# A repeated SyncE list in another order: first output weights, then loads, then the maxima's rows, and one swapped pair on ScalarE

## The chip, the core and the metric

The kernel runs on one core of a Trainium2 chip (trn2), and all of its work is one program. The metric is the device time of one execution in microseconds (us). What the measurement of this kernel can tell from no change is about 0.2%, some 2 us.

## The reference

Sixteen sequences of 256 tokens with 256 features go through four residual blocks. Cut to what matters here:

```python
x = x + einsum(x, weight[subject]) + bias[subject]                 # L0, weights chosen per sequence
x = x + zX * lap_x(x) + zY * lap_y(x) + zR * x * (1 - x)           # L1
x = x + attention(x, side, seq_len) @ Wo + bo                      # L2, 16 heads, masked softmax
s0, s1 = dense(x, swi[0], swo[0]), dense(x, swi[1], swo[1])        # L3, two shared experts
eo = relu(x @ wi[label]) @ wo[label]                               # and one chosen per sequence
w = softmax(relu(concat(eo[0], s0[0], s1[0]) @ g1) @ g2)
x = x + eo * w[0] + s0 * w[1] + s1 * w[2]
```

## The kernel before, in words

Each engine works through a list of named stages written out by hand (lines 53 to 78: `PE_BODY`, `ACT_BODY`, `DVE_BODY`, `POOL_BODY`, `SP_BODY`). An opening with lists of its own is followed by a loop over the turns i = 2 to 15, and then turns 16 and 17, in which the stages that have no sequence left are left out. One turn holds work of three sequences: the function `lag` says how far behind a stage is. `load`, `x_parts` and the other early stages are of sequence i, the attention (`S0` to `S15`, `m0`, `m1`, `E0` to `E15`) of sequence i-1, and the experts (`H0` to `H11`, `P0` to `P11`, `wi0` to `wi3`, `wo0` to `wo3`, `sum`) of sequence i-2.

The engines keep to their own lists and wait for each other by semaphores. An engine that waits holds back everything behind it in its list.

What the names of this case do:

- `load` on SyncE (SP) looks up the sequence's subject in a table in SBUF (`chooser`, line 478, a TENSOR_LOAD and register work), waits until the transfers of the last turn have read the buffers, and issues five loads: `w0_raw` (line 481; the trace calls this buffer w_raw), `x_raw` (471), `s_raw` (474), and two small ones (484, 485).
- `wo0` to `wo3` on SP each look up the chosen expert's number anew (line 478), wait until GpSimd (POOL) has finished with the quarter n of the staging buffer `raw` in this turn (its input weights, stage `wi`n), and issue one load of 256 KB into that quarter (line 494). `wi_load` fills the four quarters with the next sequence's input weights (489).
- `m0` and `m1` on SP wait until ScalarE (ACT) has copied the transposed maxima of eight heads into `max_rows` (ACT's stage of the same name, line 997), and then issue the transfer of these rows into `q_rows` (539). PE's scores `E0` to `E7` need the first transfer (line 774), `E8` to `E15` the second.
- On ACT, `wo`n and `wi`n make the high part of a quarter (`exp_hi`, line 1027), and POOL makes the low part (`exp_lo`, 1364). `x_parts`, `w_parts` and `s_parts` make the high parts of what `load` brought (929, 932, 935). `H`n is the relu of a hidden bank (1049). `P3` copies an expert's output (1034). `E`h is two exponentials of a bank of scores (1006, 1010); the end of the second one frees the bank for PE.
- On PE, `S`, `m` and `E` and the other front stages use two PSUM banks in turn, by their order in `PE_BODY`. `E0`, `E1` and `E2` share one bank and `S12`, `S13` the other one, so that `E1` on PE waits for ACT's second exponential of `E0`, and `E2` for that of `E1`. The function `open_bank` sets these waits. All other engines' lists stay as they are.

Of the kernel before, what the change touches and what calls it, by code (L numbers as in the profile page):

```python
# [60 lines left out]
vs aT ks gate wo logits vp self  # L61
""".split()
ACT_BODY = """
H0 wi0 H1 x3_keep wi1 H2 wi2 wi3 H3 m0 wo0 H4 P3 wo1 x_parts H5 E0 w_parts wo2 E1 H6 E2 wo3 E3 H7 E4 E5 E6 m1 H8 s_parts E7
x1_parts react P7 q E8 H9 E9 x2_parts qa E10 E11 H10 E12 kp E13 E14 E15 H11 qb kq P11
aT vs ks x3_parts logits vp x2b sum
""".split()
# [6 lines left out]
wi0 wi1 wi2 wi3 wo0 m0 x_parts wo1 E0 w_parts wo2 E2 wo3 E4 E6 s_parts x1 E8 m1 E9 E10 qa E12 norm E15 qb ks vp sum  # L74
""".split()
SP_BODY = """
load wo0 wo1 wo2 m0 wo3 m1 wi_load E15 kp k3 sum
""".split()

S_OF, E_OF = [f"S{h}" for h in range(H)], [f"E{h}" for h in range(H)]  # L80
# [1428 lines left out]
```

## Time and profile before

| | us |
|---|---|
| median of 3 runs (1006.3 to 1008.48) | 1006.84 |
| the profiled execution's own time | 1013.26 |
| its span in the profile | 1011.4 |
| PE busy in the span | 979.8 |
| DVE, ACT, POOL busy | 792.5, 686.3, 636.5 |

The profiled execution is 6.4 us longer than the median of the timed runs, and its span covers all but 1.9 us of it. A turn of the loop takes some 59.2 us. Times in the trace are from the span's start. In the waits, the instruction named first is the one that waited, then who released it, the sum in us, how often, and the longest.

### The profile page before, as it was taken

What the parts mean: (1) busy time and instruction counts of PE and PEld (TensorE: products, weight loads), DVE (VectorE), ACT (ScalarE), POOL (GpSimd) and SP (SyncE); (2) the same over time, 40 slices, a digit from 0 to 9 for tenths busy, and PEclk for the clock granted to TensorE, in tenths of its full rate; (3) what the DMA queues carried; (4) which work ended last, traced back from release to release, by engine and by line L of the source; (5) the groups of instructions that cost most, each with busy time, mean ns of one, the idle gap of its engine ahead of it and who ended that gap; (6) DMA issues with size and microseconds to landing.
All of it is one profiled execution on the core that took longest, in us unless ns stands there. A gap on an engine that the chain in (4) does not pass through costs nothing.

```text
span 1011.4 us, 27951 instructions
## 1 busy us (share of the span) xinstructions
PE 979.8 (97%) x9604; PEld 932.6 (92%) x9604; DVE 792.5 (78%) x1558; ACT 686.3 (68%) x1443; POOL 636.5 (63%) x546
## 2 busy tenths in 40 slices
PE   8889999999999999999999999999999999999896
PEld 7679999999999999999999999999999999999796
DVE  5877878878788787878878787887878788888533
ACT  4766858667685876768587676857767685776541
POOL 4867747576684757658575765856576585656450
PEclk8889999999999999999999999999999999999988
DMA  6533132223213222331322233133222313221110
GB/s 196 150 105 106 50 111 73 63 84 100 88 43 110 77 63 84 94 94 42 104 84 63 84 88 100 42 97 90 63 84 79 109 42 92 84 75 55 43 52 11
DMA packets 92028, 82.70 MB, mean 82 GB/s; under 512 B 12100, under 2 KB 90980, under 8 KB 92004
## 3 DMA queue, kind: packets, MB, share of 16 engines
q1 hardware_dynamic: 91572, 81.99, 27.7%
q10 hardware_dynamic: 432, 0.39, 0.1%
q8 instruction: 15, 0.25, 0.1%
q14 instruction: 9, 0.07, 0.0%
HBM read 52.59 MB, written 4.20 MB: 56 GB/s over the span
## 4 chain that ended last, share of the span: by engine, by line
POOL 35%; issue 29%; PE 26%; DVE 3%; ACT 2%; SPq 1%; DMA 1%; POOLq 1%; DVEq 0%; ACTq 0%
POOL prob_lo L1428 11%; POOL exp_lo L1364 9%; PE out L652 3%; PE out L653 3%; PE out L654 3%; PE hid L652 2%; PE hid L653 2%; PE hid L654 2%; POOL p_lo L1381 2%; POOL s_lo L1381 2%; PE front L652 2%; PE front L654 2%; PE front L653 2%; POOL beside L1384 2%; POOL ksT L1395 2%
## 5 line engine op out<-in xcount | busy, mean ns | idle before, releaser
L652 PE MATMUL hid<-x_hi,exp_hi 128*128 128x256 f32 x768 | 231.5, 301 | 1.5 <-DVE x_lo L1250 1.5
L1428 POOL TENSOR_TENSOR prob_lo<-prob,prob_hi 128x512 f16<-128x512 f32 x143 | 185.0, 1294 | 74.3 <-ACT prob_hi L1010 74.1
L652 PE MATMUL out<-hid_hi,exp_hi 128*128 128x256 f32 x768 | 226.6, 295 | 0.1
L653 PE MATMUL hid<-x_lo,exp_hi 128*128 128x256 f32 x768 | 217.2, 283 | 0.0
L654 PE MATMUL hid<-x_hi,exp_lo 128*128 128x256 f32 x768 | 216.7, 282 | 0.0
L653 PE MATMUL out<-hid_lo,exp_hi 128*128 128x256 f32 x768 | 214.6, 279 | 0.0
L654 PE MATMUL out<-hid_hi,exp_lo 128*128 128x256 f32 x768 | 214.5, 279 | 0.0
L1364 POOL TENSOR_TENSOR exp_lo<-raw,exp_hi 128x512 fp32r<-128x512 f32 x128 | 168.8, 1334 | 72.1 <-ACT exp_hi L1027 72.0
L1170 DVE TENSOR_REDUCE s_max<-front 128x2 f32<-128x512 f32 x247 | 163.3, 688 | 61.6 <-PE front L760 59.6
L1049 ACT ACTIVATE hid_hi<-hid 128x512 fp32r<-128x512 f32 x192 | 114.9, 598 | 96.3 <-PE hid L654 94.4
L1006 ACT ACTIVATE prob<-front 128x512 f32<-128x512 f32 x246 | 147.5, 600 | 24.0 <-PE front L774 22.3
L1254 DVE SCALAR_TENSOR_TENSOR hid_lo<-hid,hid_hi 128x512 fp32r<-128x512 f32 x192 | 131.1, 683 | 37.0 <-ACT hid_hi L1049 35.5
L652 PEld LDWEIGHTS hid<-x_hi,exp_hi 128*128 128x128 f32 x768 | 145.7, 190 | 4.5 <-DVE x_lo L1250 1.6
L652 PEld LDWEIGHTS out<-hid_hi,exp_hi 128*128 128x128 f32 x768 | 144.5, 188 | 2.5 <-DVE hid_lo L1254 0.3
L653 PEld LDWEIGHTS hid<-x_lo,exp_hi 128*128 128x128 f32 x768 | 146.2, 190 | 0.0
L654 PEld LDWEIGHTS hid<-x_hi,exp_lo 128*128 128x128 f32 x768 | 145.6, 190 | 0.0
L653 PEld LDWEIGHTS out<-hid_lo,exp_hi 128*128 128x128 f32 x768 | 144.8, 189 | 0.0
L654 PEld LDWEIGHTS out<-hid_hi,exp_lo 128*128 128x128 f32 x768 | 144.3, 188 | 0.0
L1010 ACT ACTIVATE prob_hi<-front 128x512 f16<-128x512 f32 x230 | 137.8, 599 | 0.0
L774 PE MATMUL front<-q_rows,k_rows 100*128 100x256 bf16 x492 | 118.5, 278 | 3.8 <-DMA q_rows<-max_rows 2.0
L1190 DVE TENSOR_TENSOR prob_lo<-prob,prob_hi 128x512 f16<-128x512 f32 x113 | 104.2, 922 | 17.9 <-ACT prob_hi L1010 16.7
L1027 ACT ACTIVATE exp_hi<-raw 128x512 fp32r<-128x512 f32 x128 | 79.2, 632 | 23.4 <-DMA raw<-in_wo 23.4
(241 smaller groups left out, 2334.6 us busy)
## 6 DMA issues: line engine op xcount, KB each, us to landing
raw<-in_wi SPq DMA_DIRECT2D x64, 256.0 KB, 3.7
raw<-in_wo SPq DMA_DIRECT2D x64, 256.0 KB, 2.8
q_rows<-w_raw SPq DMA_DIRECT2D x80, 128.0 KB, 2.4
k_rows<-x_raw SPq DMA_DIRECT2D x48, 128.0 KB, 2.4
k_rows<-x1T SPq DMA_DIRECT2D x45, 128.0 KB, 2.4
x_raw<-in_x SPq DMA_DIRECT2D x16, 256.0 KB, 2.9
w_raw<-in_w SPq DMA_DIRECT2D x16, 256.0 KB, 2.7
s_raw<-in_side SPq DMA_DIRECT2D x16, 256.0 KB, 3.7
```

The lines of the kernel that those rows point to most:

```text
L652: nc.tensor.matmul(acc, w_hi, a_hi, start=first, stop=False)
L653: nc.tensor.matmul(acc, w_hi, a_lo, start=False, stop=False)
L654: return nc.tensor.matmul(acc, w_lo, a_hi, start=False, stop=last)
L774: last = nc.tensor.matmul(psum[:, k * S:(k + 1) * S], k_rows[0:ROWS_EXP, h, k * P:(k + 1) * P], q_rows[0:ROWS_EXP, h, :], start=True, stop ...
L1006: last = nc.scalar.activation(prob[:, h % NPROB, :], psum[:, :], ACT.Exp, scale=SCALE)
L1010: last = nc.scalar.activation(prob_hi[:, h % NPROB, :], psum[:, :], ACT.Exp, scale=SCALE)
L1049: nc.scalar.activation(hid_hi[:, s % 2, :], hid_bank[s % 2][:, :], ACT.Relu).then_inc(hid_hi_done, 1)
L1170: nc.vector.tensor_reduce(s_max[:, :, h:h + 1], psum, AX_X, ALU.max).then_inc(freed["S"], 1)
L1190: nc.vector.tensor_tensor(prob_lo[:, h % NPROB, :], prob[:, h % NPROB, :], prob_hi[:, h % NPROB, :], ALU.subtract).then_inc(prob_split_dve, 1)
L1254: nc.vector.scalar_tensor_tensor(hid_lo[:, s % 2, :], hid_bank[s % 2][:, :], 0.0, hid_hi[:, s % 2, :].bitcast(F32), ALU.max, ALU.subtract) ...
L1364: nc.gpsimd.tensor_tensor(lo, source, hi.bitcast(F32), ALU.subtract).then_inc(w_split, 1)
L1428: nc.gpsimd.tensor_tensor(prob_lo[:, h % NPROB, :], prob[:, h % NPROB, :], prob_hi[:, h % NPROB, :], ALU.subtract).then_inc(prob_split_poo ...
```

## The change

In ACT's repeated list `x_parts` and `wo1` change places. In SP's repeated list `wo0` goes ahead of `load`, and `m0` goes ahead of `wo1` and `wo2`. The opening's lists stay, and so does every stage's code.

```diff
 ACT_BODY = """
-H0 wi0 H1 x3_keep wi1 H2 wi2 wi3 H3 m0 wo0 H4 P3 wo1 x_parts H5 E0 w_parts wo2 E1 H6 E2 wo3 E3 H7 E4 E5 E6 m1 H8 s_parts E7
+H0 wi0 H1 x3_keep wi1 H2 wi2 wi3 H3 m0 wo0 H4 P3 x_parts wo1 H5 E0 w_parts wo2 E1 H6 E2 wo3 E3 H7 E4 E5 E6 m1 H8 s_parts E7
 ...
 SP_BODY = """
-load wo0 wo1 wo2 m0 wo3 m1 wi_load E15 kp k3 sum
+wo0 load m0 wo1 wo2 wo3 m1 wi_load E15 kp k3 sum
 """.split()
```

## Rows read from the trace of the kernel before

**Rows 1.** First part of the page: busy time, share and instructions.

```profile
PE 979.8 (97%) x9604; PEld 932.6 (92%) x9604; DVE 792.5 (78%) x1558; ACT 686.3 (68%) x1443; POOL 636.5 (63%) x546
```

**Rows 2.** Busy time of each engine in one turn, granted clock, DMA share, GB/s.

```profile
499.10:558.30 59.20, 59.04 (x594) 56.51 (x593) 48.78 (x97) 42.05 (x89) 39.03 (x34) 1.00 0.28 80
```

**Rows 3.** Waits of PE and its weight loads, turns 2 to 15.

```profile
PEld front L774 <- DMA q_rows<-max_rows: 2.3, 4, 1.4
PE front L774 <- DMA q_rows<-max_rows: 1.2, 1, 1.2
```

**Rows 4.** SP in order of time, head of a turn: start, us, instruction.

```profile
501.09 0.40 SPq L481 DMA_DIRECT2D w_raw<-in_w  x1
...
503.28 0.34 SPq L485 DMA_DIRECT2D z_sb<-in_z  x1
504.56 2.78 SPq L494 DMA_DIRECT2D raw<-in_wo  x3
507.48 0.86 SPq L539 DMA_DIRECT2D q_rows<-max_rows  x1
509.67 0.39 SPq L494 DMA_DIRECT2D raw<-in_wo  x1
```

**Rows 5.** ACT in order of time, same turn; in brackets the idle time before.

```profile
505.30 0.37 ACT L997 ACTIVATE max_rows<-front 24x256 bf16<-24x256 bf16 x1 [1.34 <-PE front L766]
...
507.42 0.63 ACT L1027 ACTIVATE exp_hi<-raw 128x512 fp32r<-128x512 f32 x1 [1.64 <-DMA raw<-in_wo]
...
508.79 0.66 ACT L1034 ACTIVATE e_out<-out 128x256 f32<-128x256 f32 x2 [0.25 <-PE out L654]
509.34 0.63 ACT L1027 ACTIVATE exp_hi<-raw 128x512 fp32r<-128x512 f32 x1
509.86 0.63 ACT L929 ACTIVATE x_hi<-x_raw 128x512 fp32r<-128x512 f32 x1
...
513.34 0.62 ACT L1010 ACTIVATE prob_hi<-front 128x512 f16<-128x512 f32 x1
```

**Rows 6.** PE in order of time, same turn: the matmuls of E1 and E2.

```profile
512.14 0.39 PE L774 MATMUL front<-q_rows,k_rows 100*128 100x256 bf16 x2
...
514.02 0.39 PE L774 MATMUL front<-q_rows,k_rows 100*128 100x256 bf16 x2
```

**Rows 7.** SP's line 478 between wo0 and wo1, and between m0 and wo3 (ns).

```profile
L478 SPq TENSOR_LOAD <-label_sb x1: 272/272/272, 505.0 to 505.0; - x1
...
L478 SPq TENSOR_LOAD <-label_sb x1: 732/732/732, 508.4 to 508.4; - x1
```

**Rows 8.** Issue to landing: wo3 and wo2 of this turn, all 64 issues (line 494).

```profile
raw<-in_wo SPq DMA_DIRECT2D x1, 256.0 KB, 2.7
...
raw<-in_wo SPq DMA_DIRECT2D x1, 256.0 KB, 3.1
...
DMA to landing us min/median/max: 2.5/2.8/3.8
```

**Rows 9.** Turn 3 in order of time: ACT's last exponential of E1, PE's E2.

```profile
157.87 0.63 ACT L1010 ACTIVATE prob_hi<-front 128x512 f16<-128x512 f32 x1
...
158.55 0.39 PE L774 MATMUL front<-q_rows,k_rows 100*128 100x256 bf16 x2
```

**Rows 10.** POOL in order of time, the low parts of wi0 to wi3.

```profile
498.90 5.00 POOL L1364 TENSOR_TENSOR exp_lo<-raw,exp_hi 128x512 fp32r<-128x512 f32 x4
```

**Rows 11.** Turn 2: SP's last small load, ACT's maxima, PE's E2.

```profile
87.43 1.42 SPq L485 DMA_DIRECT2D z_sb<-in_z  x1
...
89.36 0.37 ACT L997 ACTIVATE max_rows<-front 24x256 bf16<-24x256 bf16 x1 [1.35 <-PE front L766]
...
99.35 0.39 PE L774 MATMUL front<-q_rows,k_rows 100*128 100x256 bf16 x2
```

**Rows 12.** Turn 16: ACT's maxima and the relu of H5.

```profile
920.25 0.37 ACT L997 ACTIVATE max_rows<-front 24x256 bf16<-24x256 bf16 x1 [1.26 <-PE front L766]
...
925.39 0.60 ACT L1049 ACTIVATE hid_hi<-hid 128x512 fp32r<-128x512 f32 x1 [0.47 <-PE hid L654]
```

## The prediction

> **What bounds the kernel now.** I read the busy shares first: TensorE (PE) is busy for 979.8 of 1011.4 us, the other engines for 792 us and less [rows 1]. The busy time by turn says the same of the loop: 59.04 of 59.20 us, at the full granted clock of 1.00 (2.4 GHz), while POOL works for 39 us and ACT for 42 [rows 2]. So the kernel is PE's own list, one matmul behind the other. Anything that comes earlier on another engine is worth only what PE now waits for it, and anything that comes later costs as soon as PE's small reserves are used up.
>
> What PE waits for is in the waits. In turns 2 to 15 its weight loads wait four times for the maxima's rows, 2.3 us together, 1.4 of them in turn 2 (PE itself 1.2) and 0.3 in three other turns [rows 3]. ACT's much longer wait, 1.64 us in each turn for wo0 [rows 5], makes nobody late: right after it ACT waits 0.25 us for PE again, before P3's output.
>
> Then the timelines of SP, ACT and PE side by side, since the change moves DMA issues against ACT's work. **ACT has almost no reserve at E1 and E2.** E2's matmuls start at 514.02 [rows 6], and the exponential that frees their bank ends at 513.34 + 0.62 = 513.96 [rows 5]. In turn 3 the same exponential ended at 158.50 and E2 started at 158.55, later than its turn in PE's list would have let it [rows 9]. So I take 0.05 us from an ACT end to the start of what waits for it, and E2's reserve is nearly nothing.
>
> **wo0 ahead of the loads.** It takes the place of w0 at 501.09 [rows 4]. What it must wait for, POOL's low part of wi0, is the first of four from 498.90 on, each 1.25 us, so done at 500.15 [rows 10]: no wait. It lands 3.5 us earlier, and ACT's 1.64 us of idle time goes. Worth nothing: ACT then waits for P3's output from PE instead.
>
> **The loads behind it.** One look-up and issue of a wo costs SP (2.78 - 0.38) / 2 = 1.20 us, an issue itself 0.38 [rows 4]. The five loads go 1.2 us later, the last one issued by 503.28 + 0.34 + 1.2 = 504.8. With the longest landing of any wo, 3.8 us [rows 8], all are there by 508.6, before ACT's x_hi, which comes at 509.34 at the earliest. Cost nothing. If that cover is gone, a late x_raw costs one for one, as wo1 does below.
>
> **The maxima's rows.** SP is free at 504.8, and ACT releases it at 505.30 + 0.37 = 505.67 [rows 5]. They are issued at 505.72 instead of 507.48 [rows 4], 1.8 us earlier. All of PE's wait for them goes: 0.3 us in three turns, and the one of turn 2.
>
> **wo1 and wo2 behind the rows: here is the price.** Before, wo1 was issued at about 505.76 (504.56 + 1.20), long before the rows. Now it can't be issued until ACT's m0 has released SP. From there:
> - rows issued 505.72 to 506.58 (0.86 us) [rows 4];
> - look-up and registers, 1.33 us, as between the rows' end at 508.34 and wo3 at 509.67 [rows 4]: wo1 issued at 507.91. The look-up there takes 0.73 us where it takes 0.27 behind a weight load [rows 7];
> - 2.76 us to ACT's start: wo3, issued alone behind the rows, lands in 2.7 [rows 8], and wo0 shows 0.06 more than the median landing until ACT starts (504.56 to 507.42: 2.86) [rows 4, 5]. So 510.67.
>
> ACT is ready for wo1 at 509.86, since **the swapped pair** puts x_parts into its place at 509.34 [rows 5] and hides 0.52 us. It idles 0.81 us. From wo1's start to the end of E1's last exponential ACT has a solid row of work: before, 509.34 to 513.96, less the 0.52 of x_hi that is now ahead of it: 4.10 us. So that end comes at 514.77 and E2 on PE at 514.82 instead of 514.02: **0.80 us lost in a turn.** E1's stall is part of this and not added. Behind E2 all is as before, only later: each engine takes its pace from PE and nothing gives it back.
>
> wo2 is issued at 509.11 and lands by 512.3 at 3.1 us [rows 8]; ACT wants it at 513.3 or so. wo3 at 510.3 is in time too. POOL's list is unchanged: it gets x_hi earlier and wo1 later and has 20 us of idle time in a turn [rows 2]; nothing.
>
> **The bounds of a turn's price.** With a look-up of 0.27 and a landing of 2.5 it is 0.80 - 0.46 - 0.20 = 0.14 us; with a landing of 3.1 it is 1.20, with 3.8 it is 1.90 [rows 7, 8]. I take 0.80, since both terms come from rows with the same neighbour, the transfer of the maxima's rows just ahead.
>
> The Trainium skill (DMA: Bandwidth & Descriptors, Anatomy of one DMA) gives 2.0 us and the bytes over 436 GB/s for a transfer, for a DMA issued by GpSimd; for 256 KB that is 2.6 us, an estimate. The trace has 2.7 for the nearest one, and by the skill's figure a turn would lose 0.1 us less.
>
> **The sum.**
> - turns 3 to 15: 13 x 0.80 = +10.4; three of them had a wait of 0.3 for the rows, which the new chain takes in: -0.9;
> - turn 2: released at 89.73, so E2 at 89.73 + 0.05 + 0.86 + 1.33 + 2.76 + 4.10 + 0.05 = 98.88 instead of 99.35, a gain of 0.47 [rows 11]. The last small load took 1.42 us there instead of 0.34, and with wo0 ahead SP may come to m0 up to 0.3 us late: I take -0.3;
> - turn 16, without x_parts to cover: released at 920.62, wo1 there at 925.62 by the same steps, H5 on ACT 0.52 later, 926.14 instead of 925.39 [rows 12]; less E1's small reserve +0.7;
> - turn 17 has no m0, no load: nothing.
>
> Together +9.9 us. The profiled execution (1013.26 us, span 1011.4) would come to 1023.2; its extra over the median belongs to both kernels, so the median goes from 1006.84 to 1016.7.
>
> **Rivals.**
> 1. *Faster: wo1 comes in time.* What decides is whether wo1 is there some 4.2 us after ACT's release (509.86 - 505.67); the rows give 5.0. If look-up and landing were both at their lower ends, 4.3, PE would keep its list, the waits for the rows would go, 1.2 + 0.9 = 2.1 us, and perhaps the last idle hundredths before E0: 1004.7. For it: that stall is real. Against: 0.73 us stands in the row with just this neighbour. Chance 0.06.
> 2. *The short look-up.* Only the look-up is 0.27: a turn loses 0.34, 13 x 0.34 - 0.9 - 0.8 + 0.2 = +2.9: 1009.7; with a landing of 2.6 too it comes within 0.2%. Chance 0.10 for the two, most of it above 0.2%. [...]
> 3. *More than a wait for one load:* wo1 shares the queue with wo2 and takes 3.1 us to land: 13 x 1.20 - 0.9 + 0.1 + 1.1 = +15.9, 1022.7. For it: wo2 took 3.1 with the rows behind it. Against: two loads were in flight ahead of wo2, and nothing is ahead of wo1. Chance 0.12.
> 4. *ACT isn't in the way.* Another buffer frees E1's bank, or the waits overlap so that the change does nothing: 1006.8. Against: turn 3's E2. Chance 0.05.
>
> My forecast keeps 0.67. The range takes in most of rival 2 and goes most of the way to rival 3: 1009.0 to 1021.5. A difference below 0.2% (2 us) couldn't be told from none. Faster 0.06, same 0.08, slower 0.86.
>
> **What would show it.** Right: ACT's waits no longer list exp_hi behind the transfer at wo0 but at wo1, about 0.8 us in each turn, with the row of idle time behind x_hi; PE waits for prob_hi at E1 or E2, 0.6 to 0.8 us, in 14 turns; a turn of 60.0 us; SP's rows 0.05 us behind ACT's max_rows; no wait for the rows. Wrong: no wait of ACT for raw behind x_hi, or a turn of 59.2 us or less. If ACT waits as said and PE doesn't, the step from ACT to E2 is what failed; if wo1's issue comes less than 2.2 us behind the release, it is the look-up.

## The result, and the profile after

| | before | after |
|---|---|---|
| median, us (runs; lowest to highest) | 1007.76 (6; 1006.3 to 1011.33) | 1017.59 (6; 1016.26 to 1019.96) |
| profiled execution, us | 1013.26 | 1018.05 |
| its span, us | 1011.4 | 1016.2 |
| 13 turns of the loop in that span, us | 770.50 | 778.41 |

The ratio is 1.0085 with a 95% interval of 1.0068 to 1.0103: slower by 0.85%, some 8.6 us, and clear of the 0.2% that can be told. The forecast was 1016.7 us, 9.9 us more than before. In this table the kernel before has six timed executions, the three of the first table among them.

The page's first part shows PE still as the bound, busy for 2.1 us less in a span that is 4.8 us longer:

```profile
PE 977.7 (96%) x9604; PEld 928.6 (91%) x9604; DVE 769.5 (76%) x1558; ACT 690.6 (68%) x1443; POOL 629.9 (62%) x546
```

One turn, busy time of each engine, clock, DMA share and GB/s, to be read beside [rows 2]: PE has 0.54 us of idle time where it had 0.16.

```profile
501.23:560.95 59.72, 59.18 (x594) 56.45 (x594) 47.00 (x97) 42.40 (x89) 38.42 (x34) 1.00 0.27 80
```

How long a turn is can be read from SP's store of the output (line 556), once a turn. Its first and its fourteenth start, 13 turns apart, in the kernel before:

```profile
143.63 0.42 SPq L556 DMA_DIRECT2D out<-e_out  x1
...
914.13 0.42 SPq L556 DMA_DIRECT2D out<-e_out  x1
```

and in the changed kernel:

```profile
141.76 0.42 SPq L556 DMA_DIRECT2D out<-e_out  x1
...
920.17 0.43 SPq L556 DMA_DIRECT2D out<-e_out  x1
```

770.50 / 13 = 59.27 us a turn before and 778.41 / 13 = 59.88 after: 0.61 us more, 7.9 in all. The span grew by only 4.8, since in this execution of before the stretch up to the first store was 1.9 us longer and the one behind the fourteenth 1.2. Those two stretches also differ between executions of one kernel: the first store of the kernel that was run twice, e10 and e12 (below), came at 141.27 and 142.93. So turns are compared below by 13 of them in the profile, and kernels by the timed ratio.

The waits of turns 2 to 15, PE and its weight loads, then ACT's for the transfers:

```profile
PE front L774 <- ACT prob_hi L1010: 7.8, 14, 1.1
PEld front L774 <- ACT prob_hi L1010: 13.1, 28, 1.3
...
ACT exp_hi L1027 <- DMA raw<-in_wo: 9.4, 15, 1.2
```

The wait for the maxima's rows [rows 3] is gone from these turns. In its place PE waits for ACT's exponential, once in each of 14 turns (its weight loads twice), and ACT's wait for the weights, 1.64 us before in the turn of [rows 5], is 9.4 us in 15 waits, 0.6 each, and it now stands at wo1 and no longer at wo0. SP at the head of a turn, as in [rows 4]:

```profile
503.21 0.41 SPq L494 DMA_DIRECT2D raw<-in_wo  x1
504.54 0.37 SPq L481 DMA_DIRECT2D w_raw<-in_w  x1
...
506.69 0.34 SPq L485 DMA_DIRECT2D z_sb<-in_z  x1
507.81 0.86 SPq L539 DMA_DIRECT2D q_rows<-max_rows  x1
510.00 2.82 SPq L494 DMA_DIRECT2D raw<-in_wo  x3
```

and ACT in the same turn, as in [rows 5]:

```profile
507.42 0.37 ACT L997 ACTIVATE max_rows<-front 24x256 bf16<-24x256 bf16 x1 [1.34 <-PE front L766]
...
510.90 0.66 ACT L1034 ACTIVATE e_out<-out 128x256 f32<-128x256 f32 x2 [1.35 <-PE out L654]
511.45 0.64 ACT L929 ACTIVATE x_hi<-x_raw 128x512 fp32r<-128x512 f32 x1
512.54 0.63 ACT L1027 ACTIVATE exp_hi<-raw 128x512 fp32r<-128x512 f32 x1 [0.46 <-DMA raw<-in_wo]
...
516.03 0.62 ACT L1010 ACTIVATE prob_hi<-front 128x512 f16<-128x512 f32 x1
```

PE's E1 and E2, as in [rows 6]:

```profile
514.69 0.39 PE L774 MATMUL front<-q_rows,k_rows 100*128 100x256 bf16 x2 [0.38 <-ACT prob_hi L1010]
...
516.70 0.39 PE L774 MATMUL front<-q_rows,k_rows 100*128 100x256 bf16 x2
```

The chain can be followed in these rows: ACT's max_rows ends at 507.79, SP issues the rows at 507.81 and wo1 at 510.00, ACT starts on it at 512.54 after 0.46 us of idle time, its last exponential of E1 ends at 516.65, and E2 starts at 516.70. From ACT's release to E2 that is 8.91 us; before it was 514.02 - 505.67 = 8.35.

This turn is the mildest of the loop. Over turns 3 to 15 the same stretch takes 8.91 to 9.18 us in the changed kernel, 9.05 on average. In the kernel before it is 8.34 to 8.37 us in ten of them and 8.52 to 8.58 in three. What varies in the changed kernel is wo1's landing: from its issue to ACT's start it takes 2.54 us here and up to 2.80, 2.67 on average. The slowest one, in the turn at 390 us:

```profile
390.09 2.80 SPq L494 DMA_DIRECT2D raw<-in_wo  x3
...
392.89 0.63 ACT L1027 ACTIVATE exp_hi<-raw 128x512 fp32r<-128x512 f32 x1 [0.72 <-DMA raw<-in_wo]
```

So the average turn pays 9.05 - 8.35 = 0.70 us at this place.

### The profile page after: what moved, and what is told of

It is laid out like the page before. It is cut to its first block, busy times and chain, and to the rows that moved or that the text cites. A ratio compares the mean times of both kernels' runs of the same rounds, so it can differ in the third digit from the quotient of the medians.

```text
span 1016.2 us, 27951 instructions
## 1 busy us (share of the span) xinstructions
PE 977.7 (96%) x9604; PEld 928.6 (91%) x9604; DVE 769.5 (76%) x1558; ACT 690.6 (68%) x1443; POOL 629.9 (62%) x546
## 4 chain that ended last, share of the span: by engine, by line
PE 35%; POOL 30%; issue 24%; ACT 3%; DVE 3%; DMA 2%; SPq 1%; POOLq 1%; ACTq 0%; DVEq 0%
POOL exp_lo L1364 10%; POOL prob_lo L1428 7%; PE out L652 3%; PE out L654 3%; PE out L653 3%; PE hid L652 3%; PE hid L653 3%; PE hid L654 3%; PE front L652 2%; PE front L654 2%; PE front L653 2%; PE front L774 2%; POOL beside L1384 1%; PE front L760 1%; DMA raw<-in_wo 1%
## 5 line engine op out<-in xcount | busy, mean ns | idle before, releaser
L1190 DVE TENSOR_TENSOR prob_lo<-prob,prob_hi 128x512 f16<-128x512 f32 x113 | 109.5, 969 | 19.0 <-ACT prob_hi L1010 17.7
L715 PE MATMUL pv<-v_cols,prob_hi 128*128 128x49 bf16 x1024 | 83.2, 185 | 4.6 <-DVE den L1201 2.0
```

Of the source, the lines that this page charges most:

```text
L1190: nc.vector.tensor_tensor(prob_lo[:, h % NPROB, :], prob[:, h % NPROB, :], prob_hi[:, h % NPROB, :], ALU.subtract).then_inc(prob_split_dve, 1)
```

## The experiments

All ratios are to the kernel before, which was timed again beside the runs (medians of 1008.2 to 1009.2 us). The length of a turn is 13 turns of the profile over 13, as above. For the kernel before that profile is of its slowest execution (1013.26 us), and its 59.27 us may be a little high: e5, which has the same list on SP, has 59.18.

| run | SP's head | ACT, PE's gate | ratio (95%) | a turn, us |
|---|---|---|---|---|
| before | load wo0 wo1 wo2 m0 wo3 | wo1 x_parts | 1 | 59.27 |
| the change | wo0 load m0 wo1 wo2 wo3 | x_parts wo1 | 1.0085 (1.0068 to 1.0103) | 59.88 |
| e1 | wo0 load wo1 wo2 m0 wo3 | as the change | 0.9975 (0.9964 to 0.9986) | 59.20 |
| e2 | load wo0 m0 wo1 wo2 wo3 | as the change | 1.0081 (1.0068 to 1.0094) | 59.93 |
| e3 | wo0 load wo1 m0 wo2 wo3 | as the change | 0.9972 (0.9961 to 0.9982) | 59.16 |
| e4 | as the change, one look-up | as the change | 0.9973 (0.9960 to 0.9985) | 59.16 |
| e5 | as before | x_parts wo1 | 0.9990 (0.9978 to 1.0002) | 59.18 |
| e6 | as the change | wo1 x_parts | 1.0159 (1.0137 to 1.0180) | 60.47 |
| e7 | as the change | wo1 behind E0 | 1.0061 (1.0039 to 1.0082) | 59.78 |
| e8 | as the change, wo1 looked up twice | as the change | 1.0173 (1.0148 to 1.0198) | 60.48 |
| e9 | as the change | w_parts ahead of H5, wo1 behind E0 | 1.0127 (1.0108 to 1.0146) | 60.17 |
| e10 | as before, one look-up | as before | 0.9999 (0.9988 to 1.0010) | 59.23 |
| e11 | e4 again | | 0.9977 (0.9966 to 0.9988) | 59.14 |
| e12 | e10 again | | 0.9987 (0.9976 to 0.9999) | 59.20 |

**Which move in SP's list costs.** Two runs undo one move each, the third puts only wo1 ahead of m0.

```diff
-wo0 load m0 wo1 wo2 wo3 m1 wi_load E15 kp k3 sum
+wo0 load wo1 wo2 m0 wo3 m1 wi_load E15 kp k3 sum    (e1)
+load wo0 m0 wo1 wo2 wo3 m1 wi_load E15 kp k3 sum    (e2)
+wo0 load wo1 m0 wo2 wo3 m1 wi_load E15 kp k3 sum    (e3)
```

Expected of e1:

> The change with m0 put back behind wo2 (SP: wo0, load, wo1, wo2, m0, wo3). Theory (the price is wo1 waiting for ACT's m0, then ACT, E1, E2): wo1 is issued some 0.9 us behind the last small load, before the rows, so ACT never waits for it; the rows go out as late as before. The loss of 0.6 us a turn is gone: ratio to before 1.000, within 0.002. Rival A (the cost is the loads coming 1.2 us later, or wo0's transfer among them): the order of wo0 and the loads is as in the change, so it stays near 1.0085.

Of e2:

> The change with wo0 back behind the loads (SP: load, wo0, m0, wo1, wo2, wo3). Theory: nothing of the price hangs on wo0's place, since SP reaches m0 at about the same time and waits there for ACT; ratio 1.0085, 0.6 us a turn, ACT's idle time at wo0 back in part. Rival A: the loss is gone, ratio near 1.000.

Of e3:

> The change with wo1 alone put ahead of m0 (SP: wo0, load, wo1, m0, wo2, wo3). Theory: wo1 is issued at about 505.8 on before's clock, the rows follow at 506.2 instead of 507.48 and wo2 at 508.4, there by 511.0 where ACT wants it at 512.3. No wait at ACT, none of PE for the rows: about 1 to 2 us faster than before, ratio 0.998 to 1.000. Rival B (whatever stands behind the rows pays, wo2 as well as wo1): wo2 late, a loss of 0.3 us or more a turn, ratio above 1.004.

With m0 back in its place the loss is gone (59.20 us a turn), with wo0 back in its place it is all there (59.93). wo0's place and the later loads cost nothing: rival A falls. The ratio of e1 came out below what was expected, 0.9975 against 1.000 within 0.002, and those of e3 and e4 too (0.9972 and 0.9973, where 0.998 was the lowest expected). In e1 the rows still go out as late as before, 1.79 us behind ACT's release (499.99 + 0.37), where it was 1.81:

```profile
502.15 0.87 SPq L539 DMA_DIRECT2D q_rows<-max_rows  x1
```

So early rows aren't what makes e1 faster than before.

e3 isolates the loss to one stage: wo1 ahead of m0 or behind it makes 0.72 us a turn (59.88 against 59.16). The SP rows of e3, and ACT's:

```profile
501.58 0.38 SPq L494 DMA_DIRECT2D raw<-in_wo  x1
502.10 0.87 SPq L539 DMA_DIRECT2D q_rows<-max_rows  x1
504.27 1.61 SPq L494 DMA_DIRECT2D raw<-in_wo  x2
```

```profile
505.19 0.64 ACT L929 ACTIVATE x_hi<-x_raw 128x512 fp32r<-128x512 f32 x1
505.71 0.63 ACT L1027 ACTIVATE exp_hi<-raw 128x512 fp32r<-128x512 f32 x1
```

wo1 is issued at 501.58, 4.1 us ahead of its use, and ACT goes from x_hi to it without a wait. The rows still go out 0.57 us behind ACT's release (501.16 + 0.37), early enough for PE, whose 13 turns are all between 59.13 and 59.18 us. wo2 behind the rows is no trouble: rival B falls.

**How much of it is the look-up.** e4 looks the expert's number up once, at wo0, and keeps it; e8 looks it up twice at wo1.

```diff
+            held = {}                                                 (ahead of SP's stages)
...
                     n = int(name[2])
-                    kind = chooser(label_sb, i, wo.shape[0])
+                    if n == 0:                                        (e4, e11; e10 and e12 in the old order)
+                        held["kind"] = chooser(label_sb, i, wo.shape[0])
+                    kind = held["kind"]
...
+                    if n == 1:                                        (e8, behind the first look-up)
+                        kind = chooser(label_sb, i, wo.shape[0])
```

Expected of e4:

> The change with one look-up of the expert's number for wo0 to wo3, at wo0, kept in a register. Theory: wo1 follows the rows by about 0.1 instead of 1.33 us, lands 1.2 us earlier, before ACT is ready for it; the loss is gone, ratio 0.998 to 1.001. Rival C (the price is the place behind the rows in the transfer queue, not SP's time): ratio stays near 1.008.

Of e8:

> The change with the look-up of wo1 done twice, a dose of SP time between the rows and wo1. Theory: the second look-up costs SP 0.5 to 0.8 us (0.27 the load, the rest registers), and since ACT and then PE have no reserve left the whole of it comes out in each of 14 turns: 7 to 11 us more than the change, ratio 1.015 to 1.020. Rival D: little or nothing more.

e4 keeps m0 ahead of wo1, and the loss is gone. Its SP rows (the lines have moved by two):

```profile
501.97 0.88 SPq L541 DMA_DIRECT2D q_rows<-max_rows  x1
503.13 1.66 SPq L496 DMA_DIRECT2D raw<-in_wo  x3
```

wo1 follows the rows' start by 1.16 us where it took 2.19 in the change. That falls short of the 0.1 us behind the rows' end that I expected (it is 0.28), and is enough: wo1 is ready in time. Rival C, the place behind the rows in the queue, falls with it. e8 is the same term the other way. From the rows' end to wo1 it has 1.93 us, 0.60 more than the 1.33 of the change:

```profile
509.87 0.87 SPq L539 DMA_DIRECT2D q_rows<-max_rows  x1
512.67 1.61 SPq L494 DMA_DIRECT2D raw<-in_wo  x2
```

and a turn has 60.48 instead of 59.88 us, 0.60 more. The chain passes SP's time on one for one, and rival D falls. The two look-ups themselves, in ns as shortest, median, longest:

```profile
L478 SPq TENSOR_LOAD <-label_sb x2: 268/518/769, 510.8 to 511.9; - x2
```

The first behind the rows takes 0.77 us, the one right after it 0.27, as behind a weight load [rows 7].

**ACT's side.** e5 has the swapped pair alone, e6 SP's order alone.

```diff
-... H4 P3 x_parts wo1 H5 E0 w_parts wo2 E1 ...
+... H4 P3 wo1 x_parts H5 E0 w_parts wo2 E1 ...    (e6; e5 is the reverse, in the kernel before)
```

Expected of e5:

> The kernel before with only ACT's pair swapped (x_parts ahead of wo1), SP's list as before. Theory: both have long landed, so the order of the two ACT operations changes nothing that PE waits for: ratio 1.000, within 0.002.

Of e6:

> The change without ACT's swapped pair (SP's new order, ACT's old one: wo1 ahead of x_parts). Theory: ACT reaches wo1 0.5 us earlier and waits for it 1.0 instead of 0.5 us, and x_parts then comes behind it, so E1 and E2 are 0.5 us later than in the change: 1.1 us a turn, ratio 1.014 to 1.016. Rival D (ACT's place in the list has no part in it): ratio 1.0085 as the change.

The pair alone moves nothing that the timing can tell. With SP's order it hides about what the prediction put it down for, 0.52 us (rival D falls here too): without it ACT idles for 1.12 us at wo1,

```profile
514.51 0.63 ACT L1027 ACTIVATE exp_hi<-raw 128x512 fp32r<-128x512 f32 x1 [1.12 <-DMA raw<-in_wo]
```

and a turn costs 1.20 us more than before, 0.59 more than the change.

**Taking wo1 out of ACT's way.** e7 leaves SP's list as the change has it and lets ACT do wo1 later.

```diff
-... H4 P3 x_parts wo1 H5 E0 w_parts wo2 E1 ...
+... H4 P3 x_parts H5 E0 wo1 w_parts wo2 E1 ...    (e7)
+... H4 P3 x_parts w_parts H5 E0 wo1 wo2 E1 ...    (e9)
```

> The change with ACT's wo1 moved on behind E0 (x_parts, H5, E0, wo1, w_parts), SP's list as in the change. Theory: wo1 has landed when ACT comes to it, H5 and E0 are not held back; POOL's E0 comes some 0.7 us later and has room. The loss is gone though SP is unchanged, and so are the waits for the rows: ratio 0.998 to 1.001. Rival C (the transfers themselves disturb PE): ratio stays near 1.008.

This expectation failed: 59.78 us a turn. ACT no longer waits for the transfer in any turn but one (0.3 us), yet E2 waits for ACT:

```profile
515.57 0.39 PE L774 MATMUL front<-q_rows,k_rows 100*128 100x256 bf16 x2 [0.46 <-ACT prob_hi L1010]
```

From ACT's release to E2 it is 8.86 us in this turn (506.71 to 515.57), one operation more than the 8.34 of a kernel without the loss. Three operations of 0.52 us now stand between the exponentials of E0 and E1, where there were two. I had looked at the wait and not at the row of work: E2's bank is freed at the end of it, so an operation put into it costs as a wait does. So e9 takes w_parts out ahead, where ACT waited for H5.

> SP's list as in the change; on ACT wo1 behind E0 as in the run that moved it there, but w_parts ahead of H5, so that only two operations of 0.52 us stand between E0 and E1, as before. Theory as mended (ACT's row of work from E0 to E1 is the gate: what stands in it, waiting or working, comes out at E1 or E2): no wait for wo1, no extra operation in the row, so the loss is gone: a turn of 59.2 us, ratio 0.997 to 0.999. Rival C (the transfers behind the rows disturb PE by themselves): a turn of 59.7 us or more, ratio 1.006 or more.

This expectation failed too, and by its numbers alone rival C would stand (60.17 us, 1.0127). The rows show another cause. The gate at ACT is open: in e9 ACT's max_rows ends at 507.23 and E2 starts at 515.57, 8.34 us later, as the 8.35 of before, with no wait. (That E2 starts at 515.57 in e7 too is chance.) But PE then waits 5.5 us further on, in 14 turns, 11.8 us in all, for the low parts of the exponentials that POOL makes in its stage E2. That is 0.84 us a turn, of the 0.90 by which the turn is longer than before, so little is left for a disturbance by the transfers, and e4, with its transfers in the same order, has no loss:

```profile
515.57 0.39 PE L774 MATMUL front<-q_rows,k_rows 100*128 100x256 bf16 x2
...
521.07 0.20 PE L715 MATMUL pv<-v_cols,prob_hi 128*128 128x49 bf16 x1 [0.84 <-POOL prob_lo L1428]
```

```profile
514.10 1.29 POOL L1364 TENSOR_TENSOR exp_lo<-raw,exp_hi 128x512 fp32r<-128x512 f32 x1 [1.21 <-ACT exp_hi L1027]
515.34 1.16 POOL L1428 TENSOR_TENSOR prob_lo<-prob,prob_hi 128x512 f16<-128x512 f32 x1
516.46 1.74 POOL L1381 TENSOR_TENSOR p_lo<-w_raw,p_hi 128x512 fp32r<-128x512 f32 x1
518.15 1.29 POOL L1364 TENSOR_TENSOR exp_lo<-raw,exp_hi 128x512 fp32r<-128x512 f32 x1
519.41 1.60 POOL L1428 TENSOR_TENSOR prob_lo<-prob,prob_hi 128x512 f16<-128x512 f32 x1
```

POOL's list has wo1 ahead of E0. It gets wo1 late and then has a solid row of five operations, the last of which ends at 521.01, 0.06 us before PE goes on. POOL idles for a third of a turn (38.42 us of work in the 59.72 of the change), and still has no reserve in this stretch. That the order of POOL's list is the cause is read from these rows: a list with POOL's wo1 behind E2 wasn't tried.

**What is left to win.** Three kernels come out ahead of both: e1, e3 and e4. e10 asks whether wo0's place has a part in that. It is the kernel before, with one look-up.

> The kernel before, both lists in their old order, with one look-up of the expert's number for wo0 to wo3. SP is through with wo2 some 1.6 us earlier and waits for ACT's m0, so the rows go out at 505.7 on before's clock instead of 507.48. Theory: this is all that the early rows are worth, with no price: PE's waits for the rows are gone, a turn of 59.16 us, turn 2 shorter by about 1 us, ratio 0.997 to 0.999, as the runs with wo1 ahead of m0 and with one look-up in the new order. Rival E (wo0 ahead of the loads is itself worth something): ratio 1.000 with the rows early.

This expectation failed: the ratio is 0.9999, as rival E had it, and the turn 59.23 us. The rows go out 0.65 us behind ACT's release in the turn at 503 us, not right behind it. Since e4 and e10 had been timed on different chips, both were timed again on one:

> The kernel of the run with one look-up in the change's order, again, beside the one with one look-up in the old order, on the same chip. If the 0.3% that three kernels with wo0 first won over the kernel before belongs to the order (rival E), this one stays at 0.997 and the other at 1.000. If it was the chip and the hour, both come to the same ratio within 0.001.

> The kernel before with one look-up, again. Rival E: 1.000 while the new order with one look-up is at 0.997. Theory: by the profiles the two differ by 0.06 us a turn and about 0.5 us in turn 2, together 1.3 us, so 0.001 between them and both at or below 1.000.

0.9977 and 0.9987: 0.1% apart, with overlapping intervals, as the profiles' 13 turns (0.06 us each, 0.8 in all) would have it. The ratio of the same kernel moved from 0.9999 (e10) to 0.9987 (e12), so a difference of 0.1% between kernels is not settled here, and neither is rival E. That the new order with one look-up, or with wo1 ahead of m0, is faster than the kernel before by 0.2 to 0.3% is settled: e3, e4 and e11 have all their intervals below 0.999. Why it is faster stays open. Early rows can't be the whole of it, as e1 shows, and by the profiles a turn of e1 (59.20 us) is no shorter than one of e5 or e12 (59.18 and 59.20), which win less.

## Why the prediction was right

- **PE is the bound, with no reserve behind ACT at E1 and E2.** Right: every run that lengthens ACT's row from its release to E2 lengthens the turn, by 0.60 us for 0.60 in e8.
- **wo0 ahead, the loads 1.2 us later: nothing.** Right, by e2 (59.93 against 59.88).
- **The chain of a turn, 8.35 + 0.80.** The places were right and the size a little large: 9.05 us on average instead of 9.15, a price of 0.70 instead of 0.80. SP woke 0.03 us behind ACT where I had taken 0.05, rows and look-up took 0.86 + 1.32 against a forecast of 0.86 + 1.33, ACT's row from wo1 to the end of E1 4.11 where I had 4.10, E2 0.05 behind. The term that was mis-sized is the landing: I took wo3's 2.7 and 0.06 more, 2.76; wo1 took 2.67 on average from issue to ACT's start, and 2.54 in the turn shown. The trace after has for wo1 alone, in the turn shown and in the one at 390 us:

```profile
raw<-in_wo SPq DMA_DIRECT2D x1, 256.0 KB, 2.5
...
raw<-in_wo SPq DMA_DIRECT2D x1, 256.0 KB, 2.8
```

  The median of the 13 turns is 2.6 us. With it the trace agrees with the 2.6 us which the Trainium skill's formula gave (DMA: Bandwidth & Descriptors, Anatomy of one DMA), an estimate from a formula for another issuing engine.
- **The waits for the rows, 0.3 us in three turns and one in turn 2.** They went, but were a little smaller: in three turns of before E2 comes 0.2 us late, 0.6 in all, where I had counted 0.9. The profile of before has some 0.6 us more in its 13 turns that these waits don't explain. e5, with the same list on SP, is without it, and against e5 the change costs just the 0.70 us a turn of the chain (59.88 against 59.18).
- **Turn 2, -0.3 us.** It was nothing: SP came to m0 0.60 us late (88.46, where ACT released it at 87.49 + 0.37 = 87.86), not 0.3, so from release to E2 it took 9.65 us, as the 9.62 of before [rows 11]. One of the loads again had a long issue there, now the third (s_raw, 1.48 us) in place of the last (1.42).
- **Turn 16, +0.7.** Nearly right at its place: from ACT's release to E2 it takes 8.92 us (926.65 to 935.57) instead of 8.32 (920.62 to 928.94), 0.60 more. The turn as a whole has only 0.2 more in the profile, but its length differs by more than 2 us between other kernels (53.5 to 55.9).
- **The sum,** +9.9, against +7.9 in the loop's 13 turns and +8.6 by the ratio: that is, for the 13 turns, 13 times 0.70 less 1.2 in place of 13 times 0.80 less 0.9, 7.9 instead of 9.5. Turns 2 and 16 should have added 0.4. That the ratio comes closer to +9.9 than the loop's turns do is not settled by any row; that the profile of before is of a slow execution may be part of it.
- **The rivals.** The short look-up was ruled out by 0.74 us in the same place in the trace after:

```profile
L478 SPq TENSOR_LOAD <-label_sb x1: 742/742/742, 508.7 to 508.7; - x1
```

  The one that expected a faster kernel named the right point: with wo1 there in time (e3, e4) the kernel is 0.2 to 0.3% faster, about its 2.1 us. Its reason for the gain, the waits for the rows, isn't shown, since e1 gains as much with late rows. The one with wo1 at 3.1 us fell by the landings of 2.5 to 2.8, the one in which ACT isn't in the way by PE's 14 waits for it.
- **POOL.** "It gets x_hi earlier and wo1 later and has 20 us of idle time in a turn; nothing" held for the change: the waits of PE's weight loads for POOL are 2.2 us in 14 turns, and were 2.1 in 13. The reason given doesn't carry, though: in e9 the same idle share covers nothing between wo1 and E2.

## What to carry to other kernels

In an engine's list a wait is a gate for all that stands behind it: before a stage that waits for the present turn's work is moved up (m0), move or shorten what is needed soon behind it (wo1, its look-up), and put behind it only what has slack (wo2). Read the reserve of a bank or a buffer at the end of the whole row of work that frees it, work and waits alike, and at the place in the turn, not from an engine's share of idle time. When an early transfer ends a wait that PE doesn't share, like ACT's 1.64 us for wo0, don't count on it: here wo0's place made no difference between the change and e2.

## What the runs showed of the hardware

A register look-up on SP takes 0.74 us right behind the issue of the maxima's rows in the changed kernel (0.73 before [rows 7]) and 0.27 right behind another look-up or a weight load. e8 has both in one stretch. Why it is longer behind the rows isn't shown. The time from the rows' end to wo1's issue, which e4 cuts from 1.33 to 0.28 us by leaving out the look-up and its register work, decides whether wo1's place behind m0 costs anything: the whole 0.72 us is gone, although the transfers go out in the same order (e4).

One 256 KB load lands in 2.5 to 2.8 us with nothing ahead of it but the rows (13 turns of the changed kernel). In the turn of [rows 8] the second and third load of a group took 3.0 and 3.1; in the changed kernel's turn at 510 us wo2 and wo3, right behind wo1, took 2.7 and 3.0.
